# VectorE's node stage written out: 53 steps in a row in place of a loop over four steps

## What is computed

```python
# layer 0: edges
edge_input = concat([x[src], edge_attr_32])
messages   = gelu(edge_input @ mW1 + mb1) @ mW2 + mb2
gates      = sigmoid(gelu(edge_input @ gW1 + gb1) @ gW2 + gb2)
aggregated = segment_sum(messages * gates, dst, N)
# layer 0: nodes (the stage that is changed)
update = gelu(concat([x, aggregated]) @ uW1 + ub1) @ uW2 + ub2
h  = x + update
x1 = layernorm(x + layernorm(h) * ln_g + ln_b)
# layer 1: attention over the edges
Q, K, V = x1 @ Wq + bq, x1 @ Wk + bk, x1 @ Wv + bv
score = exp(clip(sum_per_head(K[src] * Q[dst] / sqrt(12) * (edge_attr_96 @ We + be)), -5, 5))
out = layernorm(x1 + segment_sum(V[src] * score, dst, N) / (segment_sum(score, dst, N) + 1e-6))
```

## Time and profile before

| | us |
|---|---|
| time, median of 3 runs (lowest, highest) | 1364.21 (1361.2, 1366.08) |
| the profiled execution | 1366.79 |
| its span, first to last instruction | 1365.0 |
| busy: TensorE, VectorE | 1093.2, 953.6 |
| busy: GpSimd, ScalarE | 952.1, 694.5 |

### The profile page before, as it was taken

One profiled execution on the slowest core, in us unless ns is written; L12 is line 12 of the kernel. 1 busy time (PEld: TensorE's weight loads), 2 busy tenths in 40 slices (PEclk: granted clock), 3 DMA queues, 4 the chain that ended last, 5 costly groups with the idle time before them and its releaser, 6 DMA issues. The chain is left out here.

```text
span 1365.0 us, 25730 instructions
## 1 busy us (share of the span) xinstructions
PE 1093.2 (80%) x5194; PEld 750.3 (55%) x5194; DVE 953.6 (70%) x4332; ACT 694.5 (51%) x1522; POOL 952.1 (70%) x984
## 2 busy tenths in 40 slices
PE   1699999999998888899888870678787878778770
PEld 0366666666887777777777750344444444434340
DVE  1454444443897887878888796388888887887882
ACT  1244444442376766667766676244444444444441
POOL 6577777777777776777334355767777777777775
PEclk9799999998999787998888885788888888888885
DMA  9877777643456555667555555333333333333320
GB/s 60 191 203 210 209 209 207 175 114 120 117 177 203 181 185 179 187 182 222 172 180 177 157 180 166 77 97 106 90 103 92 102 103 90 105 89 105 88 74 24
DMA packets 170236, 194.81 MB, mean 143 GB/s; under 512 B 101813, under 2 KB 115931, under 8 KB 170149
## 3 DMA queue, kind: packets, MB, share of 16 engines
q1 hardware_dynamic: 136049, 149.30, 37.3%
q0 software_dynamic: 31360, 44.13, 13.7%
q10 hardware_dynamic: 2740, 0.60, 0.4%
HBM read 101.21 MB, written 77.56 MB: 131 GB/s over the span
## 5 line engine op out<-in xcount | busy, mean ns | idle before, releaser
L378 POOL DMA_INDIRECT rows<-agg_d,dst_at x196 | 187.1, 955 | 149.0 <-DMA agg_d<-x1o 83.3
L354 POOL DMA_INDIRECT rows<-in_x,src_i x196 | 189.1, 965 | 73.1 <-issue 58.9
L363 POOL DMA_INDIRECT agg_d<-rows,put_at x196 | 195.1, 995 | 59.7 <-issue 44.8
L400 POOL DMA_INDIRECT out<-x_in,put_at x196 | 192.7, 983 | 59.7 <-issue 56.0
L390 POOL DMA_INDIRECT x_in<-agg_d,src_i x196 | 187.9, 959 | 62.8 <-issue 57.6
L608 ACT ACTIVATE x1o<-y,nshift,nscale 128x96 f32<-128x96 f32 x392 | 145.5, 454 | 106.4 <-DVE nshift L857 105.3
L646 ACT ACTIVATE x_in<-yc,cshift,cscale 128x96 f32<-128x96 f32 x196 | 75.5, 456 | 152.4 <-DVE cshift L981 129.3
L736 DVE SCALAR_TENSOR_TENSOR ps<-hidden,ps 96x512 f32<-96x512 f32 x49 | 33.9, 692 | 158.7 <-ACT hidden L587 158.7
L410 PE MATMUL ps<-ident,x_in 128*96 128x128 f32 x588 | 98.9, 313 | 52.4 <-DMA x_in<-agg_d,src_i 51.5
L471 PE MATMUL ps<-uW2s,nT 97*128 97x96 f32 x784 | 110.0, 300 | 34.0 <-ACT nT L628 33.8
L815 DVE BATCH_NORM_STATS2 bn<-ps 128x6 f32<-128x96 f32 x392 | 99.0, 258 | 53.9 <-issue 32.9
(11 more groups left out here) (126 smaller groups left out, 2342.4 us busy)
## 6 DMA issues: line engine op xcount, KB each, us to landing
agg_d<-zeros SPq DMA_DIRECT2D x40, 480.0 KB, 4.0
x_in<-in_x SPq DMA_DIRECT2D x49, 384.0 KB
agg_in<-agg_d SPq DMA_DIRECT2D x49, 384.0 KB
agg_d<-x1o SPq DMA_DIRECT2D x49, 384.0 KB
out<-oo SPq DMA_DIRECT2D x49, 384.0 KB
mask<-cont_d SPq DMA_DIRECT2D x49, 208.0 KB
ein<-rows SPq DMA_DIRECT2D x49, 192.0 KB
mask<-cont_d SPq DMA_DIRECT2D x49, 192.0 KB, 3.3
```

The lines of the kernel that those rows point to most:

```text
L354: pool.indirect_dma_start(rows[:, g * EJ + j, :], None, x, rows_at(src_i, g, j)).then_inc(xs_gathered[g % 2][j], 16)
L363: pool.indirect_dma_start(agg_d, rows_at(put_at, g, j), rows[:, g * EJ + j, :], None, bounds_check=N - 1, oob_is_err=False).then_inc(agg_a ...
L378: pool.indirect_dma_start(rows[:, g * EJ + j, :], None, x1_d, rows_at(dst_at, g, j)).then_inc(xd_gathered[g % 2][j], 16)
L400: pool.indirect_dma_start(out, rows_at(put_at, b, j), fin[:, b % XSLOTS, j, :], None, bounds_check=N - 1, oob_is_err=False).then_inc(out_s ...
```

## The change

VectorE's program for the node stage is no longer driven by `sweep` but by a Python loop, so all of its 53 steps are written out one after another with constants for the step's number. The steps themselves, their order, the waits and the values waited for are the same, and so are the programs of the other engines and VectorE's other stages.

```diff
@@ -888,7 +888,8 @@
                 dve.wait_ge(root_step, done + 3)
                 dve.scalar_tensor_tensor(mean[:, 0, :], mdif[:, 1, :], -0.5, bn[:, 1, :, 1], ALU.mult, ALU.add).then_inc(root_step, 1)
 
-            sweep(dve, 0, NGROUPS + 4, 7, 5, update_step, XSLOTS)
+            for i in range(NGROUPS + 4):
+                update_step(i, i % XSLOTS, False)
 
             def attend_step(i, s, inner):
```

## The result

The changed kernel takes 1303.53 us (median of 4 runs, 1301.91 to 1305.55) where the kernel before, on the same chip, takes 1365.14. The ratio is 0.9554, with a 95% interval of 0.9529 to 0.9579: 61.6 us or 4.5% less. The forecast was 1302.

A forecast was written before the change was run, and what follows sets the result against it. VectorE's node stage was taken as the bound, pausing at loop returns for reloaded code. 42 steps at 8.53 us (358.3) plus 2.5 for borders make 360.8 against 423.1: gain 62.3, so 1302 us from 1364.21, range 1293 to 1322.

The forecast's parts named there:

- The bound and the cause: VectorE's node loop: 58.2 us of pauses belong to the jump back, where its 300-instruction body is loaded again.
- (1): VectorE's node loop: 9 returns go, with 31.2 + 27.0 = 58.2 us of pauses, all on the path.
- (2): Node stage afterwards: VectorE stays the bound at 8.44 to 8.59 us a step; TensorE needs 7.86, ScalarE 6.8 to 6.9.
- (3): Written-out steps 7 to 46: running over 17 instruction-packet borders costs 0 to 8.3 us, taken as 0.15 each, 2.5 us.
- (4): VectorE's node loop: the 93 register instructions a turn go, but lie beside its work, so they gain nothing.
- The pace: VectorE's node stage: each of 42 steps takes 8.53 us, as an undisturbed step of the loop does.
- (5): Node stage, steps 6 to 48: 423.1 us become 360.8, a gain of 62.3 us.
- The end moved with it: GpSimd's last block starts 62.3 us earlier, near 792 us; its wait for stores falls from 83 to about 20 us.
- B: Node stage: engines meet more often and steps take 9.09 us, gain 41 or half as likely, 1313 to 1323 us; 10%.
- C: Written-out node steps: each 256 instructions of new code cost a full reload, 25 us in all, 1327 us; 5%.
- D: VectorE's node loop: the change removes no pause, since "issue" hides something other than code, 1364 us; 4%.
- E: VectorE's attention loop: moved code is reloaded each turn, 1365 to 1425 us, 5%; with one reload a turn up to 1356, 4%.

The follow-up runs named there:

- front8_b: The kernel before with eight node-stage steps written out ahead of VectorE's loop in place of seven, loop kept: 1308.9 us, ratio 0.9589.
- attend6_b: The changed kernel with VectorE's attention loop made of six steps a turn (376 instructions) in place of two: 1310.4 us, ratio 0.9597 to the kernel before.
- gps_quiet: The changed kernel with GpSimd's gathers of x1 held back until all x1 is stored, so GpSimd is silent late in the node stage: 2095 us, slow transfers.
- after_b: The changed kernel run again, unaltered, as the measure for other runs: 1305.36 us, ratio 0.9564 to the kernel before.
- after_c: The changed kernel run again, unaltered, on a chip with slow transfers: 1897.1 us, ratio 0.9863 to the kernel before.
- eps_stt: The changed kernel with two small VectorE operations (epsilon addition, scales copy) in a two-input form: 1894.6 us, ratio 0.9818 to the kernel before, slow transfers.

## Why the prediction was right, point by point

**The bound and the cause.** That the 58.2 us belong to the jump back and are code loaded again is shown: the pauses go with the place of the body alone (front8_b), and come with a body over three stretches in another loop (attend6_b), each time with 5 packets a return. It was argued, not shown, when the prediction was made: the packets of the earlier trace rows spoke for it. The remark that "a body of 128 stays loaded, one of 300 does not" was too coarse. One of 300 stays too, if it touches two stretches.

**(1) Removed.** The totals before L815 and L833 fell from 60.4 us to 0.3. With front8_b the pauses and the slow steps behind them can be priced together on the clock, with a loop kept: 1366.2 - 1308.9 = 57.3 us. The forecast had 58.2 and some 4 for them, and no wait left at a return, where front8_b has 3.3.

**(2) What is next.** VectorE stayed the bound: busy 55.70 of 56 and 40.74 of 41 us. ScalarE still waits for its nshift (71.4 us in the whole), TensorE for ScalarE's nT (14.3 us).

**(3), the borders.** They were put at 0.15 us each, 2.5 in all. They cost about 0.5 in all (two of 0.2 and 0.3 us), so this term was mis-sized by 2.0 us.

**(4), the registers.** They were put at nothing, and that step was wrong, though small. In the loop of the kernel before (step 28, undisturbed), VectorE's timeline has:

```profile
614.57 0.16 DVE L783 SCALAR_TENSOR_TENSOR nroot<-nhalf,nroot 128x24 f32<-128x24 f32 x1
614.81 0.78 DVE L833 SCALAR_TENSOR_TENSOR y<-hg,nscale,xb 128x96 f32<-128x96 f32 x3
```

And in the kernel after:

```profile
553.36 0.16 DVE L783 SCALAR_TENSOR_TENSOR nroot<-nhalf,nroot 128x24 f32<-128x24 f32 x1
553.49 0.83 DVE L833 SCALAR_TENSOR_TENSOR y<-hg,nscale,xb 128x96 f32<-128x96 f32 x3
```

L833 starts 0.24 us after L783 in the one and 0.13 in the other. So it is throughout: 0.21 to 0.24 in the undisturbed steps of the loop before (up to 0.31 in front8_b), 0.12 to 0.14 in the written-out steps 7 to 45 but one. That is 0.1 us a step, an estimated 4 us in 40 steps, and it is about the difference between the 8.53 of step 27 to 28 and the 8.42 of gps_quiet. The waits view does not show it, as it leaves out such short gaps; it was also not separated by a run of its own. The argument that 8.53 lies between two written-out steps failed because the slower of these, 8.59 (5 to 6), holds an L775 that GpSimd stretches to 0.27 us.

**The pace.** It was put at 8.53 us a step and is 8.65 on average (363.35 / 42). With GpSimd silent the same 42 steps take 355.3 us, so some 8.0 us are GpSimd's (the two runs were on different chips). Of these 5.1 can be pointed at: from 395 to 758 us 26 of L773, L775 and L777 last over 0.22 us, 5.1 us over their usual duration; the instruction behind each is late as well. Before, when GpSimd waited more, they were 16 with 2.3 us (397 to 820). The forecast had no term for this. It came out near because the free registers (4 us), the cheap borders (2 us) and GpSimd's holds (8 us) pull against each other: that is luck. The 4 us "of slow steps behind" a TensorE with a fallen clock were also read too simply: the step of 9.09 us (465.01 to 474.10) ran at a granted clock of 1.00, VectorE waited 0.53 us in it for TensorE, which was behind after the pause, and GpSimd stretched its L777 to 0.27 us. In the kernel after, with the clock at 1.00 and no return, single steps still take 9.1.

**(5) The sum.** 360.8 us were forecast for the 42 steps, 363.35 measured, 2.5 more. Another 5.2 us were won that the forecast did not have: the stage began 2.1 us earlier in this execution (L885 of step 6 at 394.77, not 396.89), and the last block was 3.1 us shorter. Both lie within what executions differ by (after_b has 501.0 for the block, front8_b 501.3), and neither was tested. So 62.3 - 2.5 + 5.2 gives the 64.9 us (rounded) between the two profiled executions; the medians are 61.6 apart, and that this is within 1 us of the forecast is in part luck.

**The end moved with it.** L390 was forecast near 792 and starts at 792.07. GpSimd's wait for stores was forecast at about 20 us and is 25.0.

**The rivals.** B (a pace of 9.09) falls: the clock stays at 1.00 in both windows, and the steps from 395 to 758 us take 8.65 on average; three of the 42 take 9.01 to 9.10. C (a full reload at each 256 instructions) falls with gps_quiet. D falls. E, slower by the moved attention loop: VectorE's wait at its returns is 8.0 us in 20, 0.4 each, as before. attend6_b shows that its mechanism is real, but needs a third stretch, which a body of 128 can't touch. It does not test E's price: there a pause came once in six steps, in E it would come once in two. On the chip of after_c, with slow transfers, the same change is worth 1.4% in place of 4.5%; that VectorE's pauses are covered there by waits for transfers is likely, but was not tested.

## What to carry to other kernels

When an engine pauses for some 3 us with "issue" as releaser at the first instruction of a loop's body, and again after a few tens of instructions, compare the packets of the instruction queue with the number of turns, and count how many stretches of 256 instructions the body touches: up to two came back for 0.4 us, three cost 3.5 us a return on average in one loop and 6.5 in the other. Moving one step out of the loop may be all that is needed (57 of 61 us here). Writing the whole stage out cost about 0.5 us at borders here, took 0.1 us a step of register work away, and does not depend on where the code lies. Before a pace is read off one step, look whether a neighbour engine stretched something in it.

## What the runs showed of the hardware

- A small tensor_scalar on VectorE with one input from SBUF (L773, L775, L777) that starts 0.55 to 0.72 us into GpSimd's indirect transfer instruction of 0.94 to 0.97 us ends with it: 0.16 us become up to 0.43 (all 32 such starts in the kernel after). One that starts 0.47 us in or earlier is not held (L773 at 421.58, 0.44 us in, took 0.16), and one that starts from 0.81 us on takes its usual 0.16 to 0.18, by when the other is over or nearly so. The form with two inputs was not held at the same place (eps_stt, 166 ns at most in 7). The Trainium skill's SBUF — State Buffer (Who interferes with whom) has the lock between VectorE's two-port modes and GpSimd, held for a whole instruction. The trace agrees on who is held, and not on the whole instruction.
- A return to a body over three stretches brings in 5 packets of 128 instructions and costs 2.9 to 4.3 us before the first instruction (15 returns in two loops), and in the node loop 2.2 to 4.0 more 27 instructions on.
- One written-out step of 54 instructions takes 8.42 or 8.43 us on VectorE in 16 steps in a row, when GpSimd is silent (gps_quiet, 939 to 1074 us).
